# Two-layer transformer block on one core: expert weights split in other stages, another order of the ternary feed-forward, and DMA transposes in the sparse experts

## What is computed

```python
def bitlinear(x, w):                     # ternary feed-forward, D = 512, 4 D hidden
    xn = layer_norm(x)
    x_hat = absmax_quant(xn)             # clip(xn * 128 / absmax, ...) scaled back
    w_hat = ternarize_weights(w)
    return einsum('bsd,od->bso', x_hat, w_hat)
x = layernorm(x + bitlinear(gelu(bitlinear(x, w_fc)), w_proj))

# linear attention: q = k = elu(heads(x @ Wqk + bqk)), v, u = silu(x @ W + b), out = u * LN(q (k^T v))

# experts: E = 16, K = 2, H = 512, I = 352
scores = softmax(x @ gate_w.T);  combine = the two best scores of each token
gu = einsum('th,ehj->etj', x, w_gate_up);  h = silu(gu[..., :I]) * gu[..., I:]
y = einsum('eti,eih,te->th', h, w_down, combine)
y = y + swiglu(x @ shared_gate_up) @ shared_down      # shared expert, inner width 2 I
```

## Time and profile before

| | us |
|---|---|
| median of 3 runs | 2030.7 (2028.61 to 2032.78) |
| the profiled execution | 2035.29 |
| its span in the profile | 2033.5 |

### The profile page before, as it was taken

How to read it: one execution, slowest core, us unless ns; L and a number is a source line. 1 busy time by engine, 2 the same in 40 slices (tenths; PEclk the granted TensorE clock), 3 DMA queues, 4 the chain that set the end, 5 groups by cost and what they waited for, 6 DMA issues and landing times. The chain is left out here.

```text
span 2033.5 us, 34164 instructions
## 1 busy us (share of the span) xinstructions
PE 1640.1 (81%) x12714; PEld 830.6 (41%) x12714; DVE 1251.4 (62%) x2115; ACT 885.3 (44%) x1500; POOL 418.5 (21%) x503
## 2 busy tenths in 40 slices
PE   0579999777999976888955976975687699999797
PEld 0453333344333332333422542543444356666464
DVE  2548989355898847888846766765654233333277
ACT  4355777524677742444325523522244133333232
POOL 0160000144000021222211222223253111111054
PEclk9789999988999998999977987987688899999899
DMA  8000000000000001544447805812288455546434
GB/s 307 1 1 2 2 2 2 1 1 1 2 2 2 2 1 27 93 78 80 86 97 272 296 1 184 301 36 83 82 190 211 163 210 215 180 158 199 156 115 135
DMA packets 155075, 202.25 MB, mean 99 GB/s; under 512 B 93994, under 2 KB 97288, under 8 KB 152096
## 3 DMA queue, kind: packets, MB, share of 16 engines
q1 hardware_dynamic: 143392, 172.54, 27.8%
q0 software_dynamic: 7344, 20.73, 3.8%
q10 hardware_dynamic: 4176, 6.82, 0.9%
HBM read 187.17 MB, written 58.63 MB: 121 GB/s over the span
## 5 line engine op out<-in xcount | busy, mean ns | idle before, releaser
L645 DVE TENSOR_REDUCE attn_mx<-attn_ps_s 128x2 f32<-128x1024 f32 (+3 forms) x304 | 342.6, 1162 | 41.8 <-PE attn_ps_s L574 38.1
L626 ACT ACTIVATE attn_prob<-attn_ps_t 128x512 f32<-128x512 f32 x576 | 312.6, 596 | 128.1 <-PE attn_ps_t L593 126.4
L1930 PE MATMUL sparse_ps_g<-wgate,sparse_xT 128*128 128x352 f16 x1128 | 186.3, 316 | 2.7 <-DVE sparse_xT L2004 2.7
L606 PE MATMUL attn_ps_o<-attn_prob,V 128*32 128x256 f32 x2304 | 174.8, 389 | 3.6 <-ACT attn_prob L626 2.7
L878 PE MATMUL ffn_ps_y<-wprojT,ffn_hT 128*128 128x512 f16 x512 | 123.6, 398 | 33.1 <-DMA ffn_hT<-ffn_h 33.0
L1930 PEld LDWEIGHTS sparse_ps_g<-wgate,sparse_xT 128*128 128x128 f16 x1128 | 105.4, 99 | 74.2 <-DVE sparse_xT L2004 24.3
L1119 PE MATMUL lin_ps_z<-w,lin_xT 128*128 128x512 f16 x576 | 135.3, 385 | 0.0
L868 PE MATMUL ffn_ps_fc<-wfcT,ffn_xT 128*128 128x512 f16 x512 | 115.2, 384 | 17.4 <-DMA ffn_xT<-ffn_x 16.3
L593 PE MATMUL attn_ps_t<-QT,KT 64*128 64x256 f16 x1152 | 112.2, 273 | 18.6 <-ACT attn_prob L626 11.4
L780 POOL TENSOR_TENSOR wo_o<-O,wo_o 128x512 f16<-128x512 f32 (+1 forms) x16 | 18.4, 1153 | 496.2 <-ACT wo_o L752 496.1
L574 PE MATMUL attn_ps_s<-KT,QT 64*128 64x512 f16 (+3 forms) x768 | 115.2, 335 | 2.1 <-DVE attn_mx L645 2.1
(11 more groups left out here) (305 smaller groups left out, 3053.7 us busy)
## 6 DMA issues: line engine op xcount, KB each, us to landing
wgate<-gate_d SPq DMA_DIRECT2D x48, 1408.0 KB, 6.5
wdown<-down_d SPq DMA_DIRECT2D x48, 768.0 KB, 7.9
lin_sp_raw<-in_L_ffn_w_gate_up_dram SPq DMA_DIRECT2D x48, 352.0 KB, 4.9
gate_d<-lin_sp_parts SPq DMA_DIRECT2D x48, 352.0 KB, 4.3
y_d<-sparse_y SPq DMA_DIRECT2D x47, 256.0 KB, 4.8
down_d<-lin_sp_parts SPq DMA_DIRECT2D x36, 256.0 KB, 5.1
gate_d<-disp_sp_parts SPq DMA_DIRECT2D x20, 352.0 KB, 9.1
lin_sp_raw<-in_L_ffn_w_down_dram SPq DMA_DIRECT2D x24, 256.0 KB, 5.4
```

What stands on the lines that cost most here:

```text
L606: last = pe.matmul(ps_o[32 * jj:32 * jj + 32, 256 * half:256 * half + 256], V[:, kt, 4 * jg + jj, :], prob[(2 * q + jj // 2) % 4][:, half, ...
L626: act.activation(prob[g % 4][:, par, :, :], ps_t[:, (2 * g + par) % 3, :, :], ACT.Exp, scale=HD ** -0.5).then_inc(exp_done, 1)
L645: dve.tensor_reduce(mx[x % 2][:, c, :, at:at + per], ps_s[:, 2 * (r % 2):2 * (r % 2) + 2, 0:per * n].rearrange("p e (h k) -> p e h k", k=n ...
L1930: last = pe.matmul(ps_g[u][n][rows, :], xT[u][:, a, k, rows], w, start=(k == 0 and i == 0), stop=(k == KC - 1 and i == 2), skip_group_chec ...
```

## The change

- In the feed-forward the list of DVE's pieces is in another order.
- `LIN_EXPERTS` goes from 6 to 7, and the split pieces in the linear stages start one iteration later on ACT and DVE. The last two experts are split in `route`, with lags 0, 2, 2 and 3 for load, high, low and store. `dispatch` splits nothing.
- The second half of the shared expert no longer goes through DRAM: `ws_g` and `ws_d` stay allocated to the end, and `sparse_experts` loads the raw weights in iteration 6 and splits them on ACT in iteration 10 and on DVE in iteration 12.
- In `sparse_experts` the gathered rows and the gated rows are turned by DMA transposes from SP. `h2` is padded from 352 to 384 columns with zeros for that. `down` runs two iterations behind `gate`, no longer one; the order on PE is gate, up, down.

```diff
-                unrolled(NT, [(5, h_clip), (8, norm), (7, residual), (1, x_norm), (4, h_stats), (5, hlo), (2, xlo), (0, x_stats)])
+                unrolled(NT, [(5, h_clip), (8, norm), (4, h_stats), (7, residual), (5, hlo), (2, xlo), (0, x_stats), (1, x_norm)])
...
-LIN_EXPERTS = 6
+LIN_EXPERTS = 7
...
-                unrolled(TB, [(0, of(xhi)), (2, of(nonlinear)), (3, of(kt_hi)), (0, split.spread(split.high, act, TB))])
+                unrolled(TB, [(0, of(xhi)), (2, of(nonlinear)), (3, of(kt_hi)), (1, split.spread(split.high, act, TB))])
...
-                unrolled(TB, [(1, of(xevac)), (2, of(features)), (3, of(kt_lo)), (0, split.spread(split.low, dve, TB))])
+                unrolled(TB, [(1, of(xevac)), (2, of(features)), (3, of(kt_lo)), (1, split.spread(split.low, dve, TB))])
...
+        split = ExpertSplit(f, m, d, 2 * LIN_EXPERTS, NE - 2 * LIN_EXPERTS)
...
-                for t in range(NT):
+                def rows(t):
                     sp.wait_ge(xl_done, t + 1)
                     sp.dma_start(x2_rows[t], x2[t % 2][:, :, :].rearrange("p a n -> p (a n)")).then_inc(stored[t % 2], 16)
+                unrolled(NT, [(0, split.spread(split.load, sp, NT)), (0, rows), (3, split.spread(split.store, sp, NT))])
+                split.wait_stored(sp)
...
-                unrolled(NT, [(0, xhi), (0, weights)])
+                unrolled(NT, [(0, xhi), (0, weights), (2, split.spread(split.high, act, NT))])
...
-                unrolled(NT, [(1, xevac), (2, levac), (0, weights)])
+                unrolled(NT, [(1, xevac), (2, levac), (0, weights), (2, split.spread(split.low, dve, NT))])
...
-        split = ExpertSplit(f, m, d, 2 * LIN_EXPERTS, NE + 1 - 2 * LIN_EXPERTS)
...
-                unrolled(NT, [(1, lambda t: half.high(act, t)), (4, split.spread(split.high, act, 10, 0, 2)), (2, lambda t: half.evacuate(act, t)),
-                              (0, lambda t: half.tanh(act, t)), (4, split.spread(split.high, act, 10, 1, 2))])
+                unrolled(NT, [(1, lambda t: half.high(act, t)), (2, lambda t: half.evacuate(act, t)),
+                              (0, lambda t: half.tanh(act, t))])
...
-                unrolled(STEPS, [(0, gates), (1, downs), (5, outputs)])
-                free = (STEPS - STREAMS) % STREAMS
-                sp.wait_ge(y_done, STEPS - STREAMS + 1)
-                sp.dma_start(m.wgate[0][free][:, :], gate_rows[NE]).then_inc(m.shared_in, 16)
-                sp.dma_start(m.wdown[0][free][:, :], down_rows[NE]).then_inc(m.shared_in, 16)
+                def shared(s):
+                    if s == 6:
+                        load_shared(sp, d, 1, raw_g, raw_d, w_in)
+
+                def xt(t):
+                    u = t % 2
+                    sp.wait_ge(x_in[u], 16 * (t // 2 + 1))
+                    after(sp, gu_done, 2 * t - 2)
+                    sp.dma_start_transpose(out=xT[u][:, :, :, :].rearrange("p a k c -> p (a k) c"),
+                                           in_=xg[u][:, :]).then_inc(xt_in[u], 16)
+
+                def ht(t):
+                    u = t % 2
+                    sp.wait_ge(hh_done, t + 1)
+                    sp.wait_ge(pad_done, 2)
+                    sp.wait_ge(hl_done, t + 1)
+                    after(sp, y_done, t - 1)
+                    sp.dma_start_transpose(out=hT[u][:, :, :, :].rearrange("p a k c -> p (a k) c"),
+                                           in_=h2[u][:, :, :].rearrange("p a n -> p (a n)")).then_inc(ht_in[u], 16)
+
+                unrolled(STEPS, [(0, gates), (1, xt), (2, downs), (0, shared), (3, ht), (6, outputs)])
...
-                unrolled(STEPS, [(2, gate), (3, tr), (2, up), (1, xt), (3, down)])
+                unrolled(STEPS, [(2, gate), (2, up), (4, down)])
...
-                unrolled(STEPS, [(2, tanh), (3, hevac), (2, hhi), (3, yevac)])
+                unrolled(STEPS, [(2, tanh), (2, hhi), (4, yevac), (0, shared)])
...
-                unrolled(STEPS, [(2, swiglu), (2, hlo), (1, xevac)])
+                unrolled(STEPS, [(2, swiglu), (2, hlo), (0, shared)])
```

96 lines of the change are left out of this document (35 added, 61 removed).

## The result

The changed kernel is slower: 2054.1 us median (2053.6 to 2054.6, 4 runs) against 2031.7 (2028.6 to 2032.8) for the kernel before in the same session, ratio 1.0113 with a 95% interval of 1.0095 to 1.0130. The profiled execution spans 2052.8 us against 2033.5. The forecast was 1972, with a range of 1940 to 2006.

The account below looks back on a forecast made before the run. It took DVE to bound the feed-forward and PE the sparse stage, with SP's stream bounding the latter after the change. Terms -13 - 12 + 12 - 27 - 18 = -58 on the median 2030.7 gave 1972 us, range 1940 to 2006.

Parts of the forecast that it names:

- Feed-forward: Ternary feed-forward: the new order fills DVE's 1.28 us idle per tile, cycles of about 14.9, -13 us.
- linear features: Two linear feature stages: projections start earlier with split pieces one iteration later, -14, the seventh expert +2, together -12 us.
- routing: Routing stage: two experts' split loads and stores delay row-store landings to 3 to 4 us, +12; stage 65 to 70 us.
- dispatch: Dispatch stage: with split pieces gone, PE's floor of 46.9 us plus 4 for POOL replaces 78.05, -27 us.
- PE's floor of 5.52: Sparse stage: PE's least time per step without the transposes, 3.58 + 1.94 us.
- SP and not PE is the bound: Sparse stage after the change: SP's in-order instructions set the step, 5.5 to 6.5 us.
- The expected -18 of the stage: Sparse stage: at a mean pitch of 6.1 us the shared half starts at 1907 instead of 1924.5.
- the term of SP's stream: Sparse stage: SP's calls, two transposes and y take 5.5 us a step at best, 6.5 with a busy queue.
- the DMA sum: Sparse stage: 189 us of today's DMA busy time plus 113 for transposes, 302 of some 300 us, full.
- half of the steps at 5.7: Sparse stage: half of the steps at 5.7 us and half at 6.5, mean 6.1.
- (c): Rival: cost moves onto the queue, sparse pitch 6.5 to 6.9 or routing at +20, 1988 to 2008 us; chance 0.24.
- (d): Rival: slower, as the sparse loop of gather, transpose and next gather grows; 2045 us at pitch 7.8; chance 0.04.

Follow-up runs that it names:

- pe_both: The changed kernel with both transposes of the sparse stage, gathered and gated rows, back on PE as before: 1984.6 us, ratio 0.9750 to the kernel before.
- ffn_order: The kernel before with only the new order of DVE's pieces in the feed-forward: 2019.6 us, ratio 0.9912 to the kernel before.
- no_fresh: The changed kernel with an all-zero table of fresh experts, so SP's instructions stay but no weights move after three steps: 2022.1 us, ratio 0.9935.
- both_deep: The changed kernel with three buffers, transposes issued earlier, owner and fresh read once a step, down a step later, shared loads at step 17: 2006.8 us, ratio 0.9840.
- no_calls: The changed kernel without any expert weight call (register reads and loads) on SP after the first three steps: 1945.2 us, ratio 0.9564.
- x_dma: Against pe_both, only the gathered rows turned by DMA from SP, the gated rows still on PE: 2010.7 us, ratio 0.9880 to the kernel before.
- h_dma: Against pe_both, only the gated rows turned by DMA from SP, the gathered rows still on PE: 1997.2 us, ratio 0.9805 to the kernel before.
- x_deep: x_dma with three buffers for xT, xg, y, transpose earlier and ahead of the gate load, one reading a step, shared loads at step 17: 1965.5 us, ratio 0.9632.

## Why the prediction was wrong

**Right.** Feed-forward (-15.4 for -13; cycles of 14.88 for 14.95), linear features (-10.5 for -12), routing (+8.5 for +12, a landing of 2.9), dispatch (-31.1 for -27, at PE's 5.86). Their sum was -40, the trace shows -48.5, and pe_both gives -51 as a time. Only the first of these was run alone (ffn_order); the others are read from the trace. One sign failed: routing was to last 65 to 70 us, and lasted 60. PE's floor of 5.52 in the sparse stage was right to the hundredth. The claim that SP and not PE is the bound was right, as was its sign: SP's instructions back to back and PE's idle put down to xT. The expected -18 of the stage still became +67.6.

**The step that failed** is the term of SP's stream, "2.8 + 1.23 + 1.1 + 0.34 = 5.5" at best and 6.5 with a busy queue. Measured: 7.17 at best and 8.0 in the mean.

| part of a step | forecast | quiet | mean |
|---|---|---|---|
| two weight calls, with issues and gaps | 2.8 | 4.1 | 4.7 |
| xt | 1.23 to 1.8 | 1.25 | 1.47 |
| ht | 1.1 to 1.6 | 1.22 | 1.40 |
| y | 0.34 | 0.57 | 0.58 |

The transposes' own issue was sized well. The calls were taken from a trace in which no transpose stood ahead of them (1.4 us), and they cost 2.01 behind a transpose and 1.63 behind y. The same instructions cost more or less with what stood ahead of them in the queue. 47 steps at 7.17 would by themselves have been 337 us instead of 287, and no_fresh, with this stream and no bytes of weights, has a stage of 357 us against 276 without the calls.

**The second failure** is the DMA sum, "302 of some 300 us: full". It should have been a bound of its own with its own number. Measured: 331 us at a share of 0.99 (both_deep), against 180 with both on PE (0.57 of 316), so the transposes cost 148 / 47 = 3.1 us of the engines a step and not 2.4. (It is a busy time beside other traffic, and may hold some waiting of packets for each other.) Without weights beside them it is about 2.7, estimated from no_calls: 0.84 x 267 = 224 us, less some 98 for the first three experts' loads, the gathers and the y stores at their rows' sizes, over 47. The stage, with two nearly full resources, did not end at the larger of the two means. I counted half of the steps at 5.7, though fresh loads reached into the next ones: 26 of 46 steps were over 7 us. The sum also had no term for PE's clock, which fell after the long waits (21 us of longer gate and up products).

**The rivals.** (c), the queue, is the mechanism that happened, but its worst step of 6.9 was too low. (d), slower by the loop of gather, xt and gather, came near the measured time (2045; by the prediction's own sum a pitch of 7.8 gives 2051) with the wrong mechanism, which is luck: SP waited for gathers for 4.6 us in all, and with no calls the same loop ran at 5.52. The chance of 0.04 for slower rested on that one mechanism; SP's own stream had no case beyond 6.9, although its parts were known only from an empty queue.

**The two rules of the Trainium skill.** By the rate in the Trainium skill's Advanced Engine Details and Errata, "X-Bar Transpose (TRN2)", 350 to 400 GB/s, the 14 blocks were an estimated 1.2 us; the runs show 2.7 to 3.1, so the measurement decides against it. The comparison in the Trainium skill's VectorE: DVE Perf Modes, "The three transpose paths", 1309 ns by DMA against 390 on TensorE for a 128x128 block, was set aside, since 8 blocks landed in 3.5 us. Its 18 us a step do not occur here. But its direction, PE for such blocks, is what the runs found for both transposes together (pe_both against the changed kernel) and for each alone with plain buffers (x_dma, h_dma); with slack DMA drew level, and with one reading the gathered rows by DMA came out 0.6% ahead.

## What to carry to other kernels

Work moved from a compute engine to a DMA queue was paid twice here: in the issuing engine's instruction stream, and in the DMA engines' time. Sum up both over the step, each against the step's floor, and take the price of every instruction on the issuing queue with the new neighbour ahead of it, since a register read that was 0.27 us may be 0.83 behind a transpose. Try a transfer that is needed within one step ahead of the large loads that are needed later, and with a third buffer: these edits together took the steps over 7 us from 18 to 5 (x_dma to x_deep), though not in both_deep, where the DMA engines were already full. When a change has several parts, the one that trades a resource should be timed alone: here the others gave 51 us, and this one cost 74.
